# Value products of two key tiles issued together, a third buffer of probabilities, and a new order in the 16-head part of a decoder kernel

## The chip, the cores and the metric

The kernel runs on one core of a Trainium2 chip. A core has TensorE (PE in the rows; its weight loads are PEld), VectorE (DVE), ScalarE (ACT), GpSimd (POOL) and SyncE (SP, which here only issues DMAs); "q" behind an engine's name (SPq) is its sequencer. TensorE writes to PSUM, which has 8 banks of 128 x 512 fp32 words. The metric is the device time of one execution in microseconds (us); lower is better.

## The reference

Eight sequences of 512 tokens, 256 features, go through self attention with 16 heads and rotary positions, cross attention with 16 heads to a second sequence, and two layers of windowed attention with a gated MLP. A layer norm stands behind each of the three. What matters here is the 16-head part:

```python
def _L0_attn_ref(x, w_qkv, w_proj):
    qkv = x @ w_qkv
    qkv = qkv.reshape(B, N, 3, H, hd).transpose(2, 0, 3, 1, 4)
    ...
    q = q * cos + _rotate_half(q) * sin
    k = k * cos + _rotate_half(k) * sin
    attn = jax.nn.softmax(jnp.einsum('bhqd,bhkd->bhqk', q, k) * scale, axis=-1)
    out = jnp.einsum('bhqk,bhkd->bhqd', attn, v)
    ...
x = _layernorm(x + _L0_attn_ref(x, L0_attn_w_qkv, L0_attn_w_proj), axis=-1)
x = _layernorm(x + _L0_xattn_ref(x, ctx_1024, ctx_1024, ...), axis=-1)
x = _layernorm(x + _L0_ffn_ref(x, ...), axis=-1)
```

Heads have 16 features (hd), H is 16, and B here is 8.

## The kernel before

**Stages.** The program is one list of stages (`STAGES`, made by `head_stages` for the 16-head part). Each stage has a function on one or more engines, and every engine runs its own functions in the order of that list. Between engines only semaphores order the work. A "batch" vb is a sequence in the self half (0 to 7, `NB` = 8) or in the cross half (8 to 15).

**One batch.** It has 16 key tiles: four groups g of four heads, times four key tiles kt of 128 keys. For each key tile there are, on TensorE:
- four `amax` matmuls (rows PS<-KS,QS): scores with queries down the partitions, from which VectorE takes the maximum of each query (MX<-PS). They belong to the next batch;
- four `score` matmuls (PS<-QS,KS): the same scores with keys down the partitions and the negated maximum as an added row. ScalarE takes their exponential into the probabilities PT (PT<-PS);
- one `pv`: the value product, four matmuls of 17 columns (16 features and a column of ones for the sum), one for each head, which lie side by side in the array (PS<-PT,VP). The trace lists each twice, since fp32 goes through in two passes. `pv` always writes bank 3. When the fourth key tile of a group is in it, ScalarE copies it to OT (`ot`).

`amax` and `score` have 64 rows each and use different halves of the array, so a pair of them runs at once. Scores run 16 key tiles (`LAG`) behind the maxima: while batch vb's maxima are taken, the scores of vb - 1 run.

**The order.** A step (one batch) has 96 places: 32 slots (half a key tile each) of three. `SELF_ORDER` and `CROSS_ORDER` are tables of (place, stage, part, k): the stage is put at this place of step vb + k. These carry all other work. On TensorE: `tr` (x turned), `rope` and `bias1` (projections of Q and K in halves: L590, 12 matmuls for a half), `val` (L636) and `proj` (L702), 24 matmuls a half, and `maxtr` (maxima turned, L661). The two halves of one projection share two banks: the second half waits until both have "crossed".

**Banks.** `BANKS` is a string of digits: the k-th fill of the 16-head part takes the k-th digit as its bank. A fill waits until the bank's last reader is done (`vacant`, semaphores drained0 to drained7). Bank 3 is `pv`'s, so seven are left.

**Heads.** `rope_out` (or `bias1_out`) copies Q or K from PSUM to the scratch TM. GpSimd turns the rope (`mix`, `mix_sum`). `heads_hi` rounds TM to fp32r in HL, `heads_lo` puts TM - high part beside it in HL. `stack` (SyncE) waits for these, and for the scores of two batches earlier, and spreads high and low parts over QS and KS by 12 DMAs a half in the self part and 6 in the cross part, ahead of them one of NM; it counts rows00 to rows11. `taken` waits for these DMAs. `maxrows` (GpSimd) gathers the maxima, `maxtr` turns them, `negmax` (ScalarE) negates them into NM, `negmax_out` (SyncE) puts them into QS. In the cross half `load_ctx` brings the context, `ctx_hi` (ScalarE) and `ctx_lo` (GpSimd) split it, and `bias1` of K waits for both `ctx_lo`.

**Waits touched.** An exponential of key tile n writes PT[:, kt % 2] and waits for `pv` of n - 2. `rope_out` and `bias1_out` wait for `heads_lo` of the batch before, `heads_hi` waits for its row DMAs (`taken`).

## Time and profile before

| | us |
|---|---|
| median of 3 runs | 2134.76 (2134.24 to 2136.74) |
| the profiled execution | 2138.61 |
| its span, first to last instruction | 2136.8 |
| TensorE busy | 2037.9 (95%) |
| VectorE busy | 1667.7 (78%) |
| ScalarE busy | 1479.9 (69%) |
| GpSimd busy | 1351.0 (63%) |
| mean granted TensorE clock | 0.974 |

The 16-head part runs from the start to about 906 us (the last value product), the rest behind it. A matmul's duration in the rows runs from its start to a modelled end and overlaps the next, so the rate of TensorE is read from starts, not from durations. Idle time of an engine that is not the bottleneck costs nothing.

### The profile page before, as it was taken

To read this page: it belongs to the slowest core of one execution; us is meant where nothing else is said; L and a number is where in the kernel's file an instruction comes from. 1 tells how busy PE (TensorE), PEld (TensorE's weight loads), DVE (VectorE), ACT (ScalarE), POOL (GpSimd) and SP (SyncE) were. 2 spreads that over 40 slices of the span, in tenths; PEclk is the share of its full clock that TensorE was granted. 3 is DMA by queue.
4 is the path that set the end of the run, shared out by engine and by line. 5 is a ranking of instruction groups with operands and counts; after the bars stand their busy time and mean duration, and the time that the engine had idled before them with its cause. 6 is when DMAs were issued, how large, how long until landed. Compare 5 with 4: busy or idle time off the path is not lost.

```text
span 2136.8 us, 47112 instructions
## 1 busy us (share of the span) xinstructions
PE 2037.9 (95%) x15216; PEld 1484.6 (69%) x15216; DVE 1667.7 (78%) x3989; ACT 1479.9 (69%) x3418; POOL 1351.0 (63%) x1378
## 2 busy tenths in 40 slices
PE   5999999999999999779999998999899999999997
PEld 4544555455555554358889897888788988887887
DVE  6888888888888888368888886655488888875775
ACT  2488788888888888737877776554277777775443
POOL 2444566544444442678998885554489888875775
PEclk8799999999999999989999999999999999999999
DMA  4233333333233343446555544200255554551211
GB/s 134 74 101 112 113 103 113 119 119 118 103 119 123 123 123 124 142 96 156 115 120 111 113 108 97 74 16 1 67 111 113 117 118 106 116 116 45 65 60 45
DMA packets 191083, 216.30 MB, mean 101 GB/s; under 512 B 24128, under 2 KB 117056, under 8 KB 190848
## 3 DMA queue, kind: packets, MB, share of 16 engines
q1 hardware_dynamic: 188288, 204.90, 36.4%
q0 software_dynamic: 2560, 8.39, 1.1%
q8 instruction: 133, 2.18, 0.4%
q14 instruction: 102, 0.84, 0.1%
HBM read 47.14 MB, written 29.89 MB: 36 GB/s over the span
## 4 chain that ended last, share of the span: by engine, by line
PE 84%; SPq 4%; DVE 4%; POOL 3%; ACT 2%; issue 2%; DMA 1%; POOLq 0%; ACTq 0%; DVEq 0%
PE PS L685 11%; PE PS L522 11%; PE PS L524 10%; PE PS L523 10%; PE PS L669 10%; PE PS L775 5%; PE PS L799 5%; PE PS L654 5%; PE PS L590 4%; PE PS L784 4%; PE PS L759 2%; SPq L1565 2%; PE PS L702 2%; PE PS L636 2%; SPq L1586 1%
## 5 line engine op out<-in xcount | busy, mean ns | idle before, releaser
L1102 DVE TENSOR_REDUCE MX<-PS 128x1 f32<-128x512 f32 x1024 | 642.9, 683 | 113.3 <-PE PS L654 106.7
L927 ACT ACTIVATE PT<-PS 128x512 f32<-128x512 f32 x1024 | 553.3, 614 | 113.9 <-PE PS L669 111.6
L669 PE MATMUL PS<-QS,KS 64*128 64x512 f32 x1024 | 366.1, 439 | 8.1 <-ACT PT L927 3.5
L654 PE MATMUL PS<-KS,QS 64*128 64x512 f32 x1024 | 353.1, 438 | 7.8 <-DMA KS<-HL 4.8
L669 PEld LDWEIGHTS PS<-QS,KS 64*128 64x128 f32 x1024 | 164.2, 185 | 262.3 <-issue 191.6
L1472 POOL TENSOR_TENSOR PB<-PB,RC 128x512 f32<-128x512 f32 (+1 forms) x256 | 273.4, 1078 | 53.6 <-DVE RC L1224 53.4
L685 PE MATMUL PS<-PT,VP 128*17 128x512 f32 x2048 | 270.3, 600 | 6.7 <-ACT OT L934 5.2
L988 ACT ACTIVATE PB<-PB,NMf 128x256 f32<-128x256 f32 (+1 forms) x512 | 245.4, 490 | 12.7 <-DVE NMf L1215 12.4
L1215 DVE CUSTOM_DVE_ANT_0 PB<-PS,mk 128x256 f32<-128x256 f32 (+1 forms) x512 | 178.3, 386 | 60.9 <-PE PS L775 54.7
L1452 POOL TENSOR_TENSOR RI<-RI,mhalf 128x8 f32<-128x8 f32 x128 | 213.3, 1666 | 10.7
L654 PEld LDWEIGHTS PS<-KS,QS 64*128 64x128 f32 x1024 | 173.3, 189 | 47.5 <-issue 32.1
L775 PE MATMUL PS<-kT,qT 128*128 128x256 f32 (+1 forms) x1024 | 174.8, 294 | 7.8 <-DMA kT<-kT 7.5
L522 PE MATMUL PS<-WQ,XT 128*128 128x512 f32 x384 | 163.1, 425 | 11.5 <-DVE kT L1201 3.8
L524 PE MATMUL PS<-WQ,XT 128*128 128x512 f32 x384 | 155.5, 405 | 0.0
L523 PE MATMUL PS<-WQ,XT 128*128 128x512 f32 x384 | 155.3, 405 | 0.0
L775 PEld LDWEIGHTS PS<-kT,qT 128*128 128x128 f32 x1024 | 141.6, 192 | 16.3 <-issue 7.0
L522 PE MATMUL PS<-HT,W 128*128 128x512 f32 x352 | 142.4, 404 | 1.4 <-POOL HT L1487 0.8
L784 PE MATMUL PS<-ident,PB 128*128 128x128 f32 x896 | 132.0, 275 | 10.9 <-POOL PB L1472 5.9
L524 PE MATMUL PS<-HT,W 128*128 128x512 f32 x352 | 139.4, 396 | 0.0
L523 PE MATMUL PS<-HT,W 128*128 128x512 f32 x352 | 139.3, 396 | 0.0
L1458 POOL TENSOR_TENSOR RA<-RA,RI 128x512 f32<-128x512 f32 x128 | 133.2, 1041 | 3.7 <-DVE RA L1195 3.4
L1000 ACT COPY PTB<-PS 128x512 f32<-128x512 f32 (+1 forms) x256 | 130.6, 543 | 4.9 <-PE PS L784 4.8
(188 smaller groups left out, 4812.9 us busy)
## 6 DMA issues: line engine op xcount, KB each, us to landing
qT<-QN SPq DMA_DIRECT2D x384, 128.0 KB
kT<-kT SPq DMA_DIRECT2D x256, 128.0 KB
od<-OT SPq DMA_DIRECT2D x64, 256.0 KB, 4.0
QS<-HL SPq DMA_DIRECT2D x96, 128.0 KB
KS<-HL SPq DMA_DIRECT2D x96, 128.0 KB
QS<-HL SPq DMA_DIRECT2D x48, 256.0 KB
KS<-HL SPq DMA_DIRECT2D x48, 256.0 KB
OC<-od SPq DMA_DIRECT2D x32, 256.0 KB
```

The lines of the kernel that those rows point to most:

```text
L522: pe.matmul(out, L[0], R[0], start=first, stop=False)
L523: pe.matmul(out, L[0], R[1], start=False, stop=False)
L524: return pe.matmul(out, L[1], R[0], start=False, stop=last)
L654: pe.matmul(PS[:, bank, :], QS[rows, s, h // 2, qt * P:(qt + 1) * P], KS[rows, s, h // 2, :], start=True, stop=True).then_inc(fills("amax" ...
L669: pe.matmul(PS[:, bank, :], KS[rows, s, pair, kt * P:(kt + 1) * P], QS[rows, s, pair, :], start=True, stop=True).then_inc(fills("score", v ...
L685: m = pe.matmul(PS[32 * hh:32 * hh + 17, 3, :], VP[:, vb % 2, kt, 4 * g + hh, :], PT[:, kt % 2, hh, :], start=kt == 0, stop=kt == 3)
L775: m = pe.matmul(out[:, h, k0:], qT[:, u % 2, x, h, hp], kT[:, hp, h, keys], start=x == 0, stop=x == 1)
L784: m = pe.transpose(PS[:, bank, (2 * h + j) * P:(2 * h + j + 1) * P], PB[:, u % 2, 2 * hp + h, j * P:(j + 1) * P], ident[:])
L927: act.activation(PT[:, kt % 2, 2 * i + half], PS[:, TURNS["score", vb, g, kt, half, i][0], :], ACT.Exp).then_inc(drains("score", vb, g, kt ...
L988: m = act.activation(p, p, ACT.Exp, bias=NMf[:, u % 2, hh:hh + 1], scale=-1.0, accum_out=SUM[:, u % 2, hh:hh + 1])
L1102: dve.tensor_reduce(MX[:, vb % 2, h // 8, qt, c:c + 1], PS[:, TURNS["amax", vb, h, qt][0], :], AX, ALU.max).then_inc(drains("amax", vb, h, ...
L1472: pool.tensor_tensor(p, p, RC[:, u % 2, h].unsqueeze(2).broadcast_to([P, 2, 256 - k0]), ALU.mult).then_inc(sem["p_scaled"], 1)
```

## The change

- `pv` of two key tiles now stand together: at every second key tile, behind the first half of its scores, the products of the two tiles before. They were single, each behind the second half of the next tile's scores.
- The probabilities have a third buffer (PT2); the exponential of n waits for `pv` of n - 3.
- The low parts of heads go to TM itself (TMr is the same memory, typed fp32r), HL keeps the high parts alone and is half as large. So `rope_out` (of tile 0) and `bias1_out` wait for the row DMAs of the batch before, instead of `heads_lo`; `heads_hi` no longer does.
- Both order tables and the bank string are new. `load_qkv` also waits for the last `val`.

```diff
+PV_SLOT = 0
...
 SELF_ORDER = (
-    (0, "ot_out", (3,), 2), (2, "val", (1,), 0), (4, "sums", (), 2), (4, "val_out", (0,), 0), (4, "val_out", (1,), 0), (5, "tr", (0,), -1),
+    (1, "rstd", (0,), 4), (2, "stats", (0,), 4), (2, "val_out", (0,), 0), (5, "val_out", (1,), 0), (7, "tr", (0,), -1), (7, "ot", (3,), 2),
...
-            if half and 0 <= n - LAG - 1 < 16 * NV:
-                p = n - LAG - 1
-                out.append(("pv", p // 16, p // 4 % 4, p % 4))
+            if half == PV_SLOT and (n - LAG) % 2 == 0:
+                out += [("pv", p // 16, p // 4 % 4, p % 4) for p in (n - LAG - 2, n - LAG - 1) if 0 <= p < 16 * NV]
...
+            TMr, = aliases(("TMr", [P, 2, 4, S], F32R))
             TM = sb("TM", [P, 2, 4, S], F32)
-            HL = sb("HL", [P, 4, 2, S], F32R)
+            HL = sb("HL", [P, 2, 2, S], F32R)
             xT = sb("xT", [P, 2, 2, S], F32R)
+            PT2 = sb("PT2", [P, 4, S], F32)
...
+        def probs(n):
+            return PT[:, n % 3] if n % 3 < 2 else PT2
...
-                    m = pe.matmul(PS[32 * hh:32 * hh + 17, 3, :], VP[:, vb % 2, kt, 4 * g + hh, :], PT[:, kt % 2, hh, :],
+                    m = pe.matmul(PS[32 * hh:32 * hh + 17, 3, :], VP[:, vb % 2, kt, 4 * g + hh, :], probs(16 * vb + 4 * g + kt)[:, hh, :],
...
             def rope_out(vb, qk, tile):
                 act.wait_ge(*filled("rope", vb, qk, tile))
-                if vb:
-                    act.wait_ge(sem["heads_lo"], n_split(vb - 1, qk, tile))
+                if vb and tile == 0:
+                    taken(act, vb - 1, 0)
...
                 act.wait_ge(*filled("bias1", vb, qk, tile))
-                act.wait_ge(sem["heads_lo"], n_split(vb - 1, qk, tile))
+                taken(act, vb - 1, tile)
...
-                if vb:
-                    taken(act, vb - 1, tile)
-                act.copy(HL[:, 2 * qk + tile, 0], TM[:, qk, tile]).then_inc(sem["heads_hi"], 1)
+                act.copy(HL[:, qk, tile], TM[:, qk, tile]).then_inc(sem["heads_hi"], 1)
...
-                if n >= 2 and half == 0 and i == 0:
-                    act.wait_ge(sem["pv"], n - 1)
+                if n >= 3 and half == 0 and i == 0:
+                    act.wait_ge(sem["pv"], n - 2)
...
             def mix(vb, qk, tile):
-                if vb == 1 and qk == 0 and tile == 0:
-                    pool.wait_ge(sem["heads_lo"], 4)
...
-                pool.tensor_tensor(HL[:, hb, 1], TM[:, qk, tile], f(HL[:, hb, 0]), ALU.subtract).then_inc(sem["heads_lo"], 1)
+                pool.tensor_tensor(TMr[:, qk, tile], TM[:, qk, tile], f(HL[:, qk, tile]), ALU.subtract).then_inc(sem["heads_lo"], 1)
...
                     for tile in range(2):
                         taken(sp, NV - 1, tile)
+                    for half in range(2):
+                        sp.wait_ge(*filled("val", NV - 1, half))
```

The big pieces that a table moves are shown by what stands in a row on an engine. On TensorE, in a stretch of batch 5 that holds nothing but scores, maxima and products, before (L669 is a score, L654 a maxima, L685 a product; drainedN is the wait for bank N):

```order
L685 MATMUL PS<-PT,VP 17x512 [waits s_drained7,s_drained5,s_drained4,s_drained0]
L685 MATMUL PS<-PT,VP 17x512 x3
L669 MATMUL PS<-QS,KS 128x512 [waits s_negmax_in,s_drained0]
L654 MATMUL PS<-KS,QS 128x512 [waits s_drained4,s_rows00]
L669 MATMUL PS<-QS,KS 128x512 [waits s_negmax_in,s_drained1]
L654 MATMUL PS<-KS,QS 128x512 [waits s_drained6,s_rows00]
L654 MATMUL PS<-KS,QS 128x512 [waits s_drained7,s_rows00]
L669 MATMUL PS<-QS,KS 128x512 [waits s_negmax_in,s_drained2]
L654 MATMUL PS<-KS,QS 128x512 [waits s_drained5,s_rows00]
L669 MATMUL PS<-QS,KS 128x512 [waits s_negmax_in,s_drained0]
L685 MATMUL PS<-PT,VP 17x512 [waits s_drained6,s_drained2,s_drained4]
L685 MATMUL PS<-PT,VP 17x512 x3
```

The same kind of stretch in the changed kernel, in the cross half (L674, L659, L690 are the same three), its last eight fills (eight more stand ahead of them) and the products:

```order
L659 MATMUL PS<-KS,QS 128x512 [waits s_drained1,s_rows10]
L674 MATMUL PS<-QS,KS 128x512 [waits s_negmax_in,s_drained2]
L659 MATMUL PS<-KS,QS 128x512 [waits s_drained6,s_rows10]
L674 MATMUL PS<-QS,KS 128x512 [waits s_negmax_in,s_drained4]
L674 MATMUL PS<-QS,KS 128x512 [waits s_negmax_in,s_drained7]
L659 MATMUL PS<-KS,QS 128x512 [waits s_drained0,s_rows11]
L674 MATMUL PS<-QS,KS 128x512 [waits s_negmax_in,s_drained5]
L659 MATMUL PS<-KS,QS 128x512 [waits s_drained2,s_rows11]
L690 MATMUL PS<-PT2,VP 17x512 [waits s_drained5,s_drained2,s_drained0,s_drained7]
L690 MATMUL PS<-PT2,VP 17x512 x3
L690 MATMUL PS<-PT,VP 17x512 [waits s_drained2,s_drained4,s_drained0]
L690 MATMUL PS<-PT,VP 17x512 x3
```

Eight fills stood between two visits of the value products, and now sixteen stand between two double visits.

On GpSimd, in the middle of a cross step, before (xT<-tab is `ctx_lo`, MB is `maxrows`):

```order
L1378 TENSOR_TENSOR xT<-tab,xT 128x512 [waits s_x_hi] x2
L1399 TENSOR_TENSOR OCr<-OC,OCr 128x512 [waits s_oc_hi]
L1387 CAST MB<-MX 128x8x4 [waits s_drained6,s_drained7,s_drained2,s_drained5,s_drained4,s_filled0,s_drained1,s_drained0]
L1389 TENSOR_TENSOR MB<-MX,MB 128x8x4 [waits s_max_parts]
L1374 TENSOR_TENSOR HL<-TM,HL 128x512 [waits s_heads_hi] x2
```

and in the changed kernel:

```order
L1377 TENSOR_TENSOR xT<-tab,xT 128x512 [waits s_x_hi]
L1386 CAST MB<-MX 128x8x4 [waits s_drained7,s_drained4,s_drained6,s_drained0,s_drained2,s_filled0,s_drained5,s_drained1]
L1388 TENSOR_TENSOR MB<-MX,MB 128x8x4 [waits s_max_parts]
L1377 TENSOR_TENSOR xT<-tab,xT 128x512 [waits s_x_hi]
L1398 TENSOR_TENSOR OCr<-OC,OCr 128x512 [waits s_oc_hi]
```

The gathering of the maxima, which stood behind both low parts of the context, now stands between them.

On SyncE, in a cross step, before (QS<-NM of L1595 and the rows behind it are `stack` of the first half, QS<-NM of L1603 is `negmax_out`):

```order
L1610 DMA od<-OT 128x512 [waits s_sums_in,s_oc_in,s_ot]
L1595 DMA QS<-NM 4x4x512 [waits s_filled5,s_heads_lo]
L1588 DMA QS<-HL 32x4x512 x3
L1588 DMA KS<-HL 32x4x512 x3
L1603 DMA QS<-NM 4x4x512 [waits s_drained6]
L1610 DMA od<-OT 128x512 [waits s_ot] x2
L1573 DMA tab<-ctxT 128x2x512 [waits s_ctx_lo]
```

and in the changed kernel (L1594 begins `stack` there, L1602 is `negmax_out`; the first row shown is that of the second half of the maxima):

```order
L1602 DMA QS<-NM 4x4x512 [waits s_drained0]
L1572 DMA tab<-ctxT 128x2x512 [waits s_ctx_lo]
L1617 DMA OC<-od 128x1x512 [waits s_oc_lo,s_ot_out1,s_ot_out0]
L1609 DMA od<-OT 128x512 [waits s_sums_in,s_oc_in,s_ot]
L1631 DMA rs<-RR 128x64 [waits s_recip_in,s_recip_rows]
L1602 DMA QS<-NM 4x4x512 [waits s_drained4]
L1594 DMA QS<-NM 4x4x512 [waits s_filled1,s_heads_lo]
L1587 DMA QS<-HL 32x4x512 x2
L1587 DMA QS<-TMr 32x4x512
L1587 DMA KS<-HL 32x4x512
L1587 DMA KS<-TMr 32x4x512
L1587 DMA KS<-HL 32x4x512
```

The rows of the first half now stand behind `negmax_out` of the first half, and the context's load behind `negmax_out` of the second.

## Rows read from the trace of the kernel before

**Rows 1.** The page: busy time of TensorE, and the chain that ended last.

```profile
PE 2037.9 (95%) x15216; PEld 1484.6 (69%) x15216; DVE 1667.7 (78%) x3989; ACT 1479.9 (69%) x3418; POOL 1351.0 (63%) x1378
...
PE 84%; SPq 4%; DVE 4%; POOL 3%; ACT 2%; issue 2%; DMA 1%; POOLq 0%; ACTq 0%; DVEq 0%
```

**Rows 2.** Windows: stretch, length, busy PE, PEld, DVE, ACT, POOL (count), PEclk, DMA.

```profile
344.60:397.50 52.90, 52.21 (x428) 27.26 (x424) 44.51 (x78) 44.30 (x90) 35.34 (x36) 1.00 0.37 112
603.90:655.10 51.20, 51.03 (x428) 26.88 (x424) 44.05 (x77) 44.67 (x88) 22.99 (x26) 1.00 0.38 117
130.00:850.00 720.00, 715.06 (x5772) 368.26 (x5770) 615.81 (x1054) 611.80 (x1214) 346.63 (x372) 1.00 0.37 116
```

**Rows 3.** Timeline of TensorE, one bare key tile: start, duration, engine, line, tiles.

```profile
366.88 1.05 PE L685 MATMUL PS<-PT,VP 128*17 128x512 f32 x8
367.86 0.50 PE L669 MATMUL PS<-QS,KS 64*128 64x512 f32 x1
...
368.20 0.39 PE L669 MATMUL PS<-QS,KS 64*128 64x512 f32 x1
...
368.44 0.39 PE L669 MATMUL PS<-QS,KS 64*128 64x512 f32 x1
...
369.05 0.50 PE L669 MATMUL PS<-QS,KS 64*128 64x512 f32 x1
369.48 1.05 PE L685 MATMUL PS<-PT,VP 128*17 128x512 f32 x8
```

**Rows 4.** Timeline of TensorE, a key tile with half a projection.

```profile
382.80 1.05 PE L685 MATMUL PS<-PT,VP 128*17 128x512 f32 x8
...
384.36 1.60 PE L702 MATMUL PS<-WO,OCr 64*128 64x256 f32 x24
...
386.02 0.39 PE L669 MATMUL PS<-QS,KS 64*128 64x512 f32 x1
386.34 1.05 PE L685 MATMUL PS<-PT,VP 128*17 128x512 f32 x8
```

**Rows 5.** Timelines of VectorE and of ScalarE in the bare key tile.

```profile
368.43 2.48 DVE L1102 TENSOR_REDUCE MX<-PS 128x1 f32<-128x512 f32 x4 [0.23 <-PE PS L654]
...
368.39 2.06 ACT L927 ACTIVATE PT<-PS 128x512 f32<-128x512 f32 x4 [0.24 <-PE PS L669]
```

**Rows 6.** Groups, 130 to 850 us: count, busy, mean ns, idle before them.

```profile
L1102 DVE TENSOR_REDUCE MX<-PS 128x1 f32<-128x512 f32 x893 | 561.9, 683 | 91.0 <-PE PS L654 85.1
L927 ACT ACTIVATE PT<-PS 128x512 f32<-128x512 f32 x894 | 484.6, 612 | 89.1 <-PE PS L669 86.8
...
L934 ACT COPY OT<-PS 128x512 f32<-128x512 f32 x56 | 33.1, 591 | 4.0 <-PE PS L685 0.8
...
L1130 DVE BATCH_NORM_STATS2 LNT<-X 128x6 f32<-128x256 f32 x48 | 17.8, 414 | 0.0
...
L1072 DVE TENSOR_TENSOR xT<-PS,xT 128x512 fp32r<-128x512 f32 x26 | 16.8, 686 | 7.9 <-ACT xT L872 7.9
```

**Rows 7.** Timelines of SyncE and ScalarE, start of a self step.

```profile
238.38 0.58 SPq L1595 DMA_DIRECT2D QS<-NM  x1
...
242.83 4.35 SPq L1586 DMA_DIRECT2D KS<-HL  x6
...
252.27 0.60 ACT L884 ACTIVATE TM<-PS 128x512 f32<-128x512 f32 x1 [0.45 <-PE PS L590]
```

**Rows 8.** Timeline of GpSimd, middle of a cross step.

```profile
629.81 1.28 POOL L1378 TENSOR_TENSOR xT<-tab,xT 128x512 fp32r<-128x512 f32 x1 [3.49 <-ACT xT L878]
...
631.33 0.26 POOL L1389 TENSOR_TENSOR MB<-MX,MB 128x32 fp32r<-128x32 f32 x1
```

**Rows 9.** Timelines of SyncE and TensorE, end of a cross step.

```profile
539.78 0.60 SPq L1595 DMA_DIRECT2D QS<-NM  x1
...
542.35 1.92 SPq L1588 DMA_DIRECT2D KS<-HL  x3
...
552.30 0.49 PE L654 MATMUL PS<-KS,QS 64*128 64x512 f32 x1
```

**Rows 10.** The page's DMA issues: KB each, median us to landing.

```profile
od<-OT SPq DMA_DIRECT2D x64, 256.0 KB, 4.0
```

100 lines of the change are left out of this document (49 added, 51 removed).

## The prediction

> **What bounds the kernel now.** I read the page first. TensorE is busy for 95% of the span, and 84% of the chain that ended last is its own work [rows 1]. The change touches only the 16-head part, so the next view is its steady stretch. From 130 to 850 us TensorE shows 715.06 of 720 us busy, at the full granted clock (1.00, the 2.4 GHz level), while VectorE has 615.81 and ScalarE 611.80 [rows 2]. "Busy" here hides waiting, so starts have to be read. One key tile of four heads is four score matmuls, four matmuls for the maxima, and one value product. In a key tile with nothing else on TensorE, products start at 366.88 and at 369.48: 2.60 us [rows 3]. The work in it is less: a pair (score and maxima, half the rows each) starts 0.24 us after the one before (368.20, 368.44), so four pairs are 0.92; the products keep the array for 0.87 (two passes). That is 1.79, and 0.81 is something else. About 0.28 of it is changing over: 0.09 before the products (386.02 + 0.23 to 386.34, [rows 4]) and 0.19 behind them (366.88 + 0.87 to 367.86 is 0.11; the pair that starts there holds its place for 0.34 instead of 0.23, [rows 3]). The remaining 0.53 is a PSUM wait: seven banks serve eight fills, so the last score (369.05) needs the bank of the first (367.86), which is free when its exponential has ended, 368.39 + 0.60 = 368.99 [rows 3, 5]. VectorE is full in such a tile as well: four maxima in 2.48 us, 0.60 apart [rows 5].
>
> In a key tile that also holds half a projection (24 matmuls, 1.4 us) the period is 382.80 to 386.34, 3.54 us: 1.79 + 1.38 + 0.37, with no bank wait [rows 4]. So there are two regimes. A bare tile is bound by banks, VectorE and ScalarE; a loaded one by TensorE, and there the idle time of the other two collects (91.0 and 89.1 us of the 720, [rows 6]). The stretch has 893 / 4 = 223 key tiles [rows 6]; the whole part has 256. A batch took 52.90 us in the self half and 51.20 in the cross half [rows 2].
>
> **Value products of two tiles together.** 256 visits become 128, so 128 changeovers of 0.28 us go, 36 us, if TensorE is the bound everywhere. In loaded stretches it is. In bare ones I walk the new chain, with t = 0 at the first pair behind a double burst. Fills are ready at 0.50; exponentials then leave every 0.49, maxima every 0.60 [rows 5]. Sixteen fills share seven banks. By the new order the fifteenth takes the bank of the eighth (the fourth maxima: 0.54 + 3 x 0.60 + 0.68 = 3.02), the sixteenth that of the tenth (the fifth exponential: 3.10). The last pair is out at 3.2; then 0.43 to the products (369.05 to 369.48, [rows 3]), 0.98 + 0.87 for both: 5.48 us for two tiles, against 5.20 now. So a bare pair of tiles loses 0.28 where a loaded pair wins 0.28 or more. A pair with one projection half now takes 3.54 + 2.60 = 6.14 and needs only 5.5. Nothing has to be hidden for the third buffer itself: it has the 8 KB a partition that the halved HL gives up, and the exponential of tile n now waits for products n - 3.
>
> **The order anew.** It decides how much of each kind there is. I cut a batch's step into the eight stretches between double bursts and took for each the largest of: TensorE's work + 0.37; ScalarE's (0.49 an exponential, 0.5 to 0.6 any other, by the 0.59 of OT); VectorE's (0.60 a maxima, 0.65 a low part, by 0.69 less overlap, 1.05 a statistics stage, two of 0.41 and two shorter); and the 5.48. [Rows 5, 6] carry these. Self step: 9.7 + 6.1 + 5.5 + 5.5 + 5.5 + 6.9 + 6.7 + 8.2 = 54. Cross step: 6.5 + 6.7 + 5.5 + 6.7 + 5.5 + 6.9 + 5.8 + 6.7 = 50.2. The same rule on the old order, tile by tile with 2.60 as the floor, gives 52.6 (row: 52.90) and 52.2 (row: 51.20). In the self step the 8.2 is VectorE with both statistics stages and both low parts of x behind one another, and next to it stand three rope halves on TensorE (9.7) in which VectorE has only 4.8; work spills over such a border, up to the banks, so I take off 1.5. That makes self batches 52.5 against 52.9, say -0.3 each for five of them. For the cross half and the mixed steps before it the rule says -2.0; I take -1.3 because of the waits of the next paragraph. Eight of these; the first two steps and the last have few such stretches and count 0.
>
> **Steps that are moved.** The low parts of heads go to TM (TMr), so rope_out and bias1_out wait for the row DMAs of the batch before, which they did not. In a self step the second half's rows are issued from 238.38 to 247.18, and the old first rope_out stood at 252.27 [rows 7]. The new one stands some three places later, behind the burst, so the wait is met: cost 0; without that cover up to 2 us a batch. Heads_hi loses the same wait: 0, it was met long before. In a cross step GpSimd now does maxrows(0) between the two ctx_lo: these took 1.28 us, maxrows about 0.5 [rows 8]. It cannot start before the 32nd maxima. By the stretches above the burst at the batch's middle starts 6.7 + 6.5 + 6.7 + 5.5 = 25.4 us into it, and VectorE is some 1.9 behind there: 27.3. So ctx_lo(1) ends at 27.3 + 0.5 + 1.3 = 29.1, where bias1 of K is due at 28.8 (the burst and six pairs): 0.3 us, between 0 and 1 a batch. TensorE waits there, and the score fills behind it. On SyncE negmax_out(0) now stands ahead of stack(0), which earlier went 39 us into the batch (539.78 to 544.27) with the first maxima of the next at 552.30 [rows 9]. Now it waits for maxtr(0): the last two stretches, 6.9 + 5.8, less the burst and two pairs (2.4) and the negation behind two exponentials (1.3), so about 9 us before the next batch; then 0.6 and 4.5 us of issues, and a store takes up to 4.0 to land [rows 10]: between 1.3 us to spare and 0.6 late, I take 0.2. Both together 0.5, rounded up to 0.7 for the later load_ctx behind negmax_out(1). The two waits of load_qkv for val cost 0: by its place that val is some 40 us old by then. Everything behind the 16-head part stands in the old order with the same tiles: 0.
>
> **The sum.** 5 x -0.3 + 8 x -1.3 = -12 us. The profiled execution took 2138.6 us (span 2136.8 and 1.8 around it), 3.9 above the median of 2134.76, so I put the difference on the median: **2123 us**.
>
> **The rivals.** (A) *TensorE's whole saving shows*: work spills freely over the borders, the 0.28 comes back 128 times, with some bank wait saved too: -24 to -40, about 2103. For it: in the loaded tiles nothing but TensorE binds [rows 4]. Against it: VectorE is full in the bare ones [rows 5]. The Trainium skill, TensorEngine Tiling (Array Packing), Key Properties, says that changing the tiling mode drains TensorE; by that rule alone this rival would be the forecast, and the trace agrees with the drain but not that it binds everywhere. (B) *The evacuation takes it back*: during a burst of 1.85 us no score is made. At its second product at most two exponentials are queued (0.98 us) against 1.5 us until the next, and VectorE's queue is 3.5 of 0.60. Bare pairs pay 0.28 four times a batch, and the crowded 8.2 stretch does not spill: self +1.3 x 5; cross (-1.3 + 4 x 0.5) x 8, where in each of four light stretches one more step of VectorE or ScalarE, 0.5 us, falls in front of the last bank: +12, 2147. It decides from the point at which a double stretch with no projection takes over 5.8 us. The same page, section PSUM Bottleneck, warns that the PSUM copy may become the limit once TensorE is faster; no figure of it is used. (C) *Late rows or late context*: TensorE waits 2.5 us instead of 0.7 in each cross batch, because GpSimd and SyncE are blocked as above (8 x (-2.0 + 2.5) = +4), and the self rows are late by 1 us (5 x (-0.3 + 1.0) = +3.5): +8, 2143. (D) *No change*: gains and losses cancel within 4.3 us.
>
> **How the numbers follow.** The forecast, -4.3 to -24: 0.48. A: 0.12. D: 0.15. B: 0.15. C: 0.10. Faster by over 0.2% (4.3 us, about what a measurement of this kernel can tell) is 0.60, within it 0.15, slower 0.25. The range is 2103 to 2147: A's middle to B; the forecast's own is 2111 to 2130.
>
> **What would show it.** After: 128 bursts of products, each 1.92 us from its first to its last matmul's end, with no gap between the two tiles (a gap would mean that exponentials are late). Bare stretches of 5.4 to 5.6 us from burst to burst; over 5.8 says B. Loaded ones of 6.6 to 6.9 with two projection halves. Cross batches near 50, self near 52.5. TensorE waiting for xT of GpSimd, or for KS and QS by DMA, for more than 5 us in all says C. What follows 906 us should take as long as before. If bare stretches stay at 5.2, the bank chain is wrong and it is A.

## The result, and the profile after

The changed kernel took 2174.48 us (median of 4 runs, 2171.94 to 2177.27) against 2135.75 us for the kernel before beside it (4 runs, 2134.24 to 2142.25): ratio 1.0179, 95% interval 1.016 to 1.0198. It is slower, by 38.7 us. The prediction of 2123 us had the sign wrong, and its range ended at 2147.

**Where the time went.** I looked first for the stage. In the kernel before, the last value product starts at 905.5 us and 1231 us follow to the end. In the changed kernel it starts at 945.6 us and 1230 us follow. So all of the loss lies in the 16-head part, and what stands behind it cost nothing, as predicted. Inside that part the first maxima of each batch give its length. In the order of the batches:

| us | self, 1 to 3 | 4 to 7 | 8 (mixed) | 9 (first context) | cross, 10 on |
|---|---|---|---|---|---|
| before | 44.8, 51.6, 51.7 | 54.4, 53.0, 52.8, 53.0 | 51.3 | 51.9 | 51.6, 51.6, 51.2, 51.5, 51.4, 51.5 |
| after | 45.9, 52.2, 53.6 | 57.3, 55.1, 55.0, 55.1 | 53.2 | 57.0 | 54.7, 54.0, 54.2, 54.1, 54.1, 54.2 |

Nearly every batch is 2 to 3 us longer, and one is 5 us longer. The loss is spread out, so it has a cause that returns in each batch.

The page after (busy time, then the share of the chain that ended last, by engine; then groups with their idle time):

```profile
PE 2062.3 (95%) x15216; PEld 1536.5 (71%) x15216; DVE 1663.1 (76%) x3989; ACT 1474.0 (68%) x3418; POOL 1350.7 (62%) x1378
...
PE 77%; DVE 5%; SPq 5%; ACT 3%; POOL 3%; DMA 3%; issue 3%; POOLq 0%; DVEq 0%; ACTq 0%
...
L1104 DVE TENSOR_REDUCE MX<-PS 128x1 f32<-128x512 f32 x1024 | 636.2, 681 | 165.1 <-PE PS L659 164.0
L930 ACT ACTIVATE PT<-PS 128x512 f32<-128x512 f32 x1024 | 550.8, 616 | 162.2 <-PE PS L674 161.7
```

Set beside [rows 1], TensorE is "busy" for 24 us more with the same instructions, its own work is 77% of the chain instead of 84%, and transfers have 3% instead of 1%. VectorE and ScalarE have as much work as before; they only wait longer for TensorE.

The windows that answer to [rows 2] (a self batch, a cross batch, the steady stretch; the columns are those of that group):

```profile
356.10:411.30 55.20, 54.08 (x426) 31.15 (x426) 44.29 (x77) 44.22 (x90) 35.27 (x37) 1.00 0.38 111
630.10:684.20 54.10, 52.53 (x424) 29.88 (x424) 44.38 (x78) 44.27 (x89) 23.03 (x26) 1.00 0.33 112
130.00:890.00 760.00, 737.78 (x5781) 416.67 (x5779) 610.22 (x1053) 605.31 (x1212) 346.03 (x372) 1.00 0.35 111
```

The granted clock is 1.00 here as in [rows 2], so the clock has no part in it.

**A bare double stretch** (timeline of TensorE, changed kernel: two key tiles with nothing else, from burst to burst; some rows left out):

```profile
652.66 1.91 PE L690 MATMUL PS<-PT,VP 128*17 128x512 f32 x16
654.50 0.49 PE L659 MATMUL PS<-KS,QS 64*128 64x512 f32 x1
...
655.31 0.39 PE L674 MATMUL PS<-QS,KS 64*128 64x512 f32 x1
655.81 0.59 PE L659 MATMUL PS<-KS,QS 64*128 64x512 f32 x2
...
657.77 0.47 PE L659 MATMUL PS<-KS,QS 64*128 64x512 f32 x1
658.17 0.62 PE L690 MATMUL PS<-PT,VP 128*17 128x512 f32 x4
```

The burst is 1.91 us for 16 passes in one piece, 1.92 was predicted. The stretch is 5.51 us, 5.48 was predicted. The step that I had worked hardest on was right, and it is a loss, as predicted: two bare tiles of the kernel before take 5.19 us.

**A loaded double stretch** (same view, two halves of a projection of 24 matmuls each, L641):

```profile
630.73 1.91 PE L690 MATMUL PS<-PT,VP 128*17 128x512 f32 x16
632.57 0.49 PE L659 MATMUL PS<-KS,QS 64*128 64x512 f32 x1
...
633.14 0.62 PE L674 MATMUL PS<-QS,KS 64*128 64x512 f32 x2
633.88 0.47 PE L659 MATMUL PS<-KS,QS 64*128 64x512 f32 x1
634.37 1.70 PE L641 MATMUL PS<-W,xT 64*128 64x256 f32 x24
635.88 0.39 PE L659 MATMUL PS<-KS,QS 64*128 64x512 f32 x1
...
636.34 1.61 PE L641 MATMUL PS<-W,xT 64*128 64x256 f32 x24
...
638.34 0.62 PE L690 MATMUL PS<-PT,VP 128*17 128x512 f32 x4
```

This one takes 7.61 us, where 6.5 to 6.9 was predicted. Read the starts: the burst and its exit take 1.84 us (to 632.57). Eight fills follow. The first pair holds its place for 0.34 us (632.57 to 632.91), three more need 0.23 each, so the projection could start 1.03 us later. It starts 1.80 us later, at 634.37. The eighth fill comes at 633.88 instead of 633.37, and the projection waits again, since it needs two banks at once. That is 0.77 us in which TensorE has no bank to write to. Behind the first half of the projection nothing waits any more: 1.51, 0.46, 1.41, 0.46 and 0.13 us. In the kernel before a projection half stood behind four fills and did not wait at all ([rows 4]: 382.80 + 0.98 + two pairs, and L702 is there at 384.36).

VectorE in the same stretch (its timeline; the bracket is the idle time before the row):

```profile
628.57 3.67 DVE L1104 TENSOR_REDUCE MX<-PS 128x1 f32<-128x512 f32 x6
...
633.10 2.48 DVE L1104 TENSOR_REDUCE MX<-PS 128x1 f32<-128x512 f32 x4
...
636.30 1.29 DVE L1104 TENSOR_REDUCE MX<-PS 128x1 f32<-128x512 f32 x2 [0.71 <-PE PS L659]
```

and ScalarE:

```profile
628.84 2.58 ACT L930 ACTIVATE PT<-PS 128x512 f32<-128x512 f32 x5
633.14 2.06 ACT L930 ACTIVATE PT<-PS 128x512 f32<-128x512 f32 x4 [1.72 <-PE PS L674]
...
636.33 1.09 ACT L930 ACTIVATE PT<-PS 128x512 f32<-128x512 f32 x2 [0.65 <-PE PS L674]
```

ScalarE has emptied its queue 0.7 us after the burst began (628.84 + 2.58 = 631.42) and idles 1.72 us. From 633.14 on it gives back a bank every 0.49 us. By the bank string the eighth fill takes the bank of the first exponential, which ends at about 633.74 (633.14 + 0.60), and the fill starts at 633.88. The projection takes the banks of the first maxima (its matmul at 632.57) and of the second exponential, which ends at about 634.23, and it starts at 634.37. So both waits end with ScalarE's first two exponentials behind the burst. VectorE isn't idle there: the rows left out at 632.15 to 633.11 are statistics. Later, during the projections, both engines idle again.

**Against the kernel before, kind by kind.** The loaded stretches are where the forecast was missed, but they aren't the only place where the change lost. In a cross batch two tiles with a half of `val` each took 7.1 to 7.3 us and now take 7.6 together. The two halves of `proj` with a `maxtr` took 7.3 to 7.8 and take 7.8. The tiles with the projections of Q and K lose 0.4 in all, those with `tr` and `maxtr` 0.5, and the three bare pairs 0.3 each, which the prediction had counted. With late rows (next) that makes the 2.4 to 3.1 us of a cross batch. A pair of tiles thus costs 0.3 us in the mean (38.7 / 128).

**Late rows, cross half** (timeline of SyncE, changed kernel, the end of a batch):

```profile
675.18 0.57 SPq L1602 DMA_DIRECT2D QS<-NM  x1
675.85 0.56 SPq L1594 DMA_DIRECT2D QS<-NM  x1
...
679.69 1.32 SPq L1587 DMA_DIRECT2D KS<-HL  x1
```

and the first maxima of the next batch on TensorE:

```profile
684.24 0.50 PE L659 MATMUL PS<-KS,QS 64*128 64x512 f32 x1 [0.44 <-DMA KS<-HL]
```

`stack` of the first half is issued from 675.85, behind `negmax_out`; its last issue ends at 681.0, and the row of TensorE says that a transfer of these rows is what it waited for until 684.24. The fill before it stood at 683.3, so 0.9 us passed without one. At the starts of batches 11 to 16 these gaps are 0.8 to 1.5 us, at that of batch 10 2.1. (With rows in time, in e8 below, they are 0.3, and 0.5 at batch 10.)

In the self half the rows are in time, but the negated maxima are not: `negmax_out` stands behind the twelve issues of `stack`. Before 465 us TensorE waits for QS<-NM by DMA 3.3 us in six times, and the last double stretch of the self batches takes 8.0 to 8.7 us, where the same work takes 7.6 in the cross half.

### The profile page after: what moved, and what is told of

The parts are those of the page before. It is cut to its first block, busy times and chain, and to the rows that moved or that the text cites. A ratio compares the mean times of both kernels' runs of the same rounds, so it can differ in the third digit from the quotient of the medians.

```text
span 2175.5 us, 47041 instructions
## 1 busy us (share of the span) xinstructions
PE 2062.3 (95%) x15216; PEld 1536.5 (71%) x15216; DVE 1663.1 (76%) x3989; ACT 1474.0 (68%) x3418; POOL 1350.7 (62%) x1378
## 4 chain that ended last, share of the span: by engine, by line
PE 77%; DVE 5%; SPq 5%; ACT 3%; POOL 3%; DMA 3%; issue 3%; POOLq 0%; DVEq 0%; ACTq 0%
PE PS L527 11%; PE PS L528 10%; PE PS L529 10%; PE PS L690 9%; PE PS L659 7%; PE PS L674 5%; PE PS L780 5%; PE PS L804 5%; PE PS L595 4%; PE PS L789 4%; PE PS L764 2%; SPq L1585 2%; DVE MX L1104 2%; DMA KS<-HL 2%; PE PS L641 2%
## 5 line engine op out<-in xcount | busy, mean ns | idle before, releaser
L1104 DVE TENSOR_REDUCE MX<-PS 128x1 f32<-128x512 f32 x1024 | 636.2, 681 | 165.1 <-PE PS L659 164.0
L659 PE MATMUL PS<-KS,QS 64*128 64x512 f32 x1024 | 375.4, 447 | 19.2 <-DMA KS<-HL 6.3
L674 PE MATMUL PS<-QS,KS 64*128 64x512 f32 x1024 | 353.8, 437 | 6.0 <-DMA QS<-NM 5.0
L659 PEld LDWEIGHTS PS<-KS,QS 64*128 64x128 f32 x1024 | 175.6, 188 | 189.1 <-issue 170.2
L690 PE MATMUL PS<-PT,VP 128*17 128x512 f32 x2048 | 249.0, 602 | 8.5 <-ACT OT L937 4.6
L674 PEld LDWEIGHTS PS<-QS,KS 64*128 64x128 f32 x1024 | 171.7, 184 | 57.2 <-issue 14.2
L690 PEld LDWEIGHTS PS<-PT,VP 128*17 128x17 f32 x2048 | 48.0, 96 | 126.4 <-issue 108.3
```

Of the source, the lines that this page charges most:

```text
L659: pe.matmul(PS[:, bank, :], QS[rows, s, h // 2, qt * P:(qt + 1) * P], KS[rows, s, h // 2, :], start=True, stop=True).then_inc(fills("amax" ...
L674: pe.matmul(PS[:, bank, :], KS[rows, s, pair, kt * P:(kt + 1) * P], QS[rows, s, pair, :], start=True, stop=True).then_inc(fills("score", v ...
L690: m = pe.matmul(PS[32 * hh:32 * hh + 17, 3, :], VP[:, vb % 2, kt, 4 * g + hh, :], probs(16 * vb + 4 * g + kt)[:, hh, :], start=kt == 0, st ...
L1104: dve.tensor_reduce(MX[:, vb % 2, h // 8, qt, c:c + 1], PS[:, TURNS["amax", vb, h, qt][0], :], AX, ALU.max).then_inc(drains("amax", vb, h, ...
```

## The experiments

All times are medians, and each ratio is to the kernel before, run on the same chip beside it. The kernel before gave 2134.5 to 2137.1 us beside them, so a difference of two experiments is known to some 3 us; where it matters, the difference by the ratios is given too. The first four cross the two parts: order tables (with their bank string), and products alone or together. All four keep the new layout, the third buffer and the new waits.

### Old order, single products (e1)

```diff
 SELF_ORDER, CROSS_ORDER, BANKS: those of the kernel before
-            if half == PV_SLOT and (n - LAG) % 2 == 0:
-                out += [("pv", ...) for p in (n - LAG - 2, n - LAG - 1) ...]
+            if half and 0 <= n - LAG - 1 < 16 * NV:
+                p = n - LAG - 1
+                out.append(("pv", p // 16, p // 4 % 4, p % 4))
```

> The order tables and the bank string of before, each value product alone, but the third buffer, the low parts over TM and their waits as in the changed kernel. Theory (the waits for PSUM banks behind a double burst cost the time): nothing but waits with room differs from before, so the time is that of before, 2131 to 2139 us. Rival (the wait of rope_out and bias1_out for the row DMAs costs it): 15 us or more above before, since in the old order the first rope_out stands some 2 us behind the landing.

Measured: 2158.22 us, 1.0104 (1.0083 to 1.0125), above what I expected: the rival was right, though through `bias1_out` alone. From the fourth to the eleventh the batches are as before; then come 56.6, 57.8, 55.7 and 57.2 us instead of 51.2 to 51.5. The waits of ScalarE from 600 to 828 us (what waited, for whom: us in total, times, longest):

```profile
ACT TM L898 <- DMA KS<-HL: 14.6, 4, 4.3
```

and those of TensorE in the same stretch:

```profile
PE PS L660 <- ACT TM L898: 14.3, 4, 4.2
```

L898 is `bias1_out` and L660 the maxima. The new layout makes it wait for the rows of the second half, which the old table issues late (`stack`(1) at place 9). The self batches from the fourth on do not change, so the wait of `rope_out` costs nothing there (the first three are 3.9 us shorter together, which I did not follow up). But my "0" for the layout held only with the new table.

### The same, with one issue moved (e5)

```diff
-(9, "stack", (1,), 0)
+(0, "stack", (1,), 0)
```

> Kernel: the two order tables, the bank string and the single value products of the kernel before, with the third buffer, the new place of the low parts and the new waits of the change; only stack(1) of the cross half goes from place 9 to place 0, so that the row transfers that bias1_out now waits for are issued some 5 us earlier. Theory (the layout costs nothing in itself; the +21 us of e1 were those late rows alone, which e1 showed as 14.6 us of waiting in 4 batches at ScalarE and as four last batches of 55.7 to 57.7 us instead of 51.5): 2137 us, between 2133 and 2142, all cross batches at 51.2 to 51.9. Rival (third buffer or the new waits of heads_hi, rope_out and bias1_out cost in every batch): 2150 or more. A third buffer that helps the single products by sparing a wait would give below 2130.

Measured: 2136.93 us, 1.0018 (1.0007 to 1.0029), as expected. One entry of the table gives back 18 us by the ratios (21 by the medians). The third buffer wins nothing for single products, and the layout costs next to nothing: the self batches from the second on have 51.0 to 54.4 us, as before or up to 0.6 less, and of the cross batches one has 53.9 and the last two 52.2 and 52.3, where `bias1_out` still waits a little for rows (TensorE waits for it 2.7 us in five times).

### Old order, products together (e2)

```diff
 SELF_ORDER, CROSS_ORDER, BANKS: those of the kernel before (products together as changed)
```

> The order tables and the bank string of before, with the value products of two key tiles together. Theory: the pairing by itself costs, because four pairs of matmuls and then a projection half follow a burst and meet seven banks: 2150 to 2185 us, with loaded stretches of 7.4 us or more. Rival (the new order costs it and the pairing gains): below before, 2105 to 2125 us.

Measured: 2303.21 us, 1.0779 (1.0759 to 1.0798), far outside of both expectations. A stretch of it (TensorE):

```profile
631.24 1.91 PE L690 MATMUL PS<-PT,VP 128*17 128x512 f32 x16
633.08 1.69 PE L707 MATMUL PS<-WO,OCr 64*128 64x256 f32 x24
...
635.80 0.47 PE L659 MATMUL PS<-KS,QS 64*128 64x512 f32 x1 [0.34 <-ACT PT L930]
...
636.42 1.77 PE L707 MATMUL PS<-WO,OCr 64*128 64x256 f32 x24
...
640.81 0.62 PE L690 MATMUL PS<-PT,VP 128*17 128x512 f32 x4
```

Here the projection stands directly behind the burst: from the burst's start no score or maxima is made for 3.4 us, and already the sixth fill behind it waits for a bank. From burst to burst it is 9.57 us for the same work and one `maxtr`, where the changed kernel takes 7.8. So a projection right behind a burst looks worse than one behind eight fills; tables and bank string differ as well, and its place was not varied alone. The new tables avoid that place; they were made for the pairs.

### New order, single products (e3)

```diff
 products as in the kernel before, and two ot entries later, behind their last product:
-(49, "ot", (1,), 1)    # self        -(26, "ot", (0,), 1)    # cross
+(54, "ot", (1,), 1)                  +(30, "ot", (0,), 1)
```

> The order tables and the bank string of the changed kernel, with each value product alone behind the second half of the next tile's scores; two entries of ot (self 1 from 49 to 54, cross 0 from 26 to 30) stand later, so that ScalarE doesn't wait for products that come later. Theory: with the bursts apart the bank waits shorten, and what is left over before are late rows in the cross half and the crowded VectorE stretch: 2140 to 2160 us. Rival (the new order is what costs): as slow as the changed kernel, 2168 us or more.

Measured: 2217.28 us, 1.0377 (1.0361 to 1.0392): a miss for the theory, the rival's side of it (2168 or more). TensorE again:

```profile
635.33 1.05 PE L691 MATMUL PS<-PT,VP 128*17 128x512 f32 x8 [1.06 <-ACT OT L938]
...
639.01 0.50 PE L675 MATMUL PS<-QS,KS 64*128 64x512 f32 x1 [0.36 <-DVE MX L1105]
```

The products wait for `ot`, 12.6 us in 13 times from 130 to 890 us, fills wait for banks another 27 us, and both halves of a projection often fall into one single tile. So the four combinations are: old order 2158 (2137 with the one entry moved) single and 2303 together; new order 2217 single and 2174 together. Each table fits its own way of placing the products, and the two halves of the change can't be added up. That says nothing yet on the pairing itself.

### Rows ahead of negmax_out (e4)

```diff
-(49, "negmax_out", (0,), 0), (50, "stack", (0,), -1)
+(79, "negmax_out", (0,), 0), (50, "stack", (0,), -1)
```

> The changed kernel with one entry moved: in the cross half negmax_out of the first half stands behind stack of the first half on SyncE (place 79 instead of 49). Theory: the first maxima of a cross batch start in the changed kernel as the rows land (684.24 us), so each of eight batches is freed of 0.5 to 1.5 us: 2162 to 2171 us. If rows are the main cause it falls to 2150 or less; if they cost nothing it stays within 3 us of 2174.

Measured: 2186.03 us, 1.0223 (1.0204 to 1.0241): a miss. The rows came in time, but the negated maxima now came behind them in SyncE's queue (waits of TensorE, 470 to 700 us):

```profile
PE PS L674 <- DMA QS<-NM: 10.7, 3, 4.5
```

It moved the lateness from one transfer to the other, and three batches around the start of the cross half became 58.7 to 59.7 us.

### Smaller rows (e8)

```diff
-                        sp.dma_start(f(T[k:P:4, vb % 2, pairs]), f((HL, TMr)[a][:, qk, half]))...
+                        few, rows = (pairs, slice(0, P)) if k < 2 else (slice(4 * half, 4 * half + 1), slice(0, 32))
+                        sp.dma_start(f(T[k:P:4, vb % 2, few]), f((HL, TMr)[a][rows, qk, half]))...
```

> The changed kernel, in which of the six row transfers of a cross half (256 KB each) the third and the sixth bring 32 KB rather than 256 (a quarter of the pairs, a quarter of the rows): a part of the operands is left out, the issues on SyncE stay. Theory (in the cross batches the rows of the next batch land too late: stack(0) is issued 45.7 to 50.9 us into the batch and lands at 54.1, where the first maxima of the next stands): 0.5 to 1.3 us less in each of 8 cross batches: 2163 to 2171 us, and TensorE's waits for KS and QS by DMA (11.4 us in 15 times) fall below 4. Rival (what ends the batch is TensorE's own time and the rows only come last by a hair): 2172 or more.

Measured: 2167.44 us, 1.0159 (1.014 to 1.0179), as expected: 7.0 us less than the changed kernel by the medians, 4.3 by the ratios, whose intervals overlap. The traces decide for the larger number: the 16-head part is 7.1 us shorter (938.5 against 945.6 us to the last product). The waits of TensorE for KS by DMA (4.5 us, and 6.9 at its weight loads) are gone but for 0.3. The batch of the first context goes from 57.0 to 53.9, the cross batches from 54.1 to 53.8. So late rows are about 7 us of the 38.7, and some 32 are left.

### Half the evacuation (e6, e7)

VectorE and ScalarE read 256 of the 512 columns in each maxima and each exponential: half of the evacuation of PSUM is left out, TensorE's work stays. e6 is the kernel before with it, e7 the changed one.

```diff
-dve.tensor_reduce(MX[...], PS[:, TURNS["amax", vb, h, qt][0], :], AX, ALU.max)
+dve.tensor_reduce(MX[...], PS[:, TURNS["amax", vb, h, qt][0], 0:256], AX, ALU.max)
...
+                w = S if n < 3 else 256
-                act.activation(probs(n)[:, 2 * i + half], PS[:, ..., :], ACT.Exp)
+                act.activation(probs(n)[:, 2 * i + half, 0:w], PS[:, ..., 0:w], ACT.Exp)
```

> Kernel before, in which each maxima (VectorE) and, from the third key tile on, each exponential (ScalarE) reads 256 of the 512 columns of its bank; half of the probabilities stay those of the first tiles. It leaves out half of this work on the two engines and nothing on TensorE. It is the partner of e7. A maxima should come every 0.33 us instead of 0.60 (the 128x256 statistics take 0.41 where 128x512 takes 0.68) and an exponential every 0.27 instead of 0.49. The bank wait of 0.53 in each bare key tile goes: some 90 to 130 tiles of 0.3 to 0.5 us, so -35 to -60: 2075 to 2100.

> The changed kernel with the same work left out as in e6 (half of each maxima and of each exponential). Theory (in a double burst VectorE and ScalarE empty their queues, and afterwards the banks come back at their pace, which makes the loaded double stretches 7.6 us long instead of 6.7 to 6.9): with both twice as fast the loaded stretches fall to 6.5 to 6.9, the bare ones to 4.2 to 4.8, and of the 38.7 us between the two kernels at most 15 remain: 2090 to 2115 us, a gain of 60 to 85 against the changed kernel. Rival (TensorE itself, its projections behind eight fills or the order, takes the 7.6): loaded stretches stay above 7.3, and the distance to e6 stays 30 us or more.

Measured: e6 2102.51 us (0.9852, 0.9835 to 0.9869), a little above its range; e7 2113.96 us (0.9895, 0.9869 to 0.992), as expected. The changed kernel gains 60 us from it, the kernel before 32, and of the 38.7 us between the two 11.5 are left. So most of what the change lost hangs on how fast banks come back, and not on TensorE's own work. The readers are not quite twice as fast: an exponential comes every 0.28 us instead of 0.49, a maxima every 0.34 to 0.37 instead of 0.60.

Stretch by stretch the pair says more. In the cross half two tiles with a half of `val` each take 3.54 + 3.54 us in e6 and 7.18 together in e7, `proj` with its `maxtr` 7.5 to 7.8 and 7.48, two bare tiles 4.76 and 4.61. So with faster readers pairing costs at most 0.1 us in a stretch, and in most it wins. What keeps e7 behind e6 is transfers, for which TensorE waits 22.5 us in 14 times (130 to 890 us), in e6 3.5 in three. The rows of e7:

```profile
PE PS L674 <- DMA QS<-NM: 11.6, 7, 2.7
PE PS L659 <- DMA KS<-HL: 10.9, 7, 2.0
```

The loaded stretch in e7 (TensorE):

```profile
557.92 1.91 PE L690 MATMUL PS<-PT,VP 128*17 128x512 f32 x16
559.76 0.50 PE L659 MATMUL PS<-KS,QS 64*128 64x512 f32 x1
...
560.92 0.47 PE L659 MATMUL PS<-KS,QS 64*128 64x512 f32 x1
561.20 1.66 PE L595 MATMUL PS<-xT,W 64*128 64x512 f32 x12
...
565.10 0.62 PE L690 MATMUL PS<-PT,VP 128*17 128x512 f32 x4
```

From burst to burst it is 7.18 us, where I had set at most 6.9. From the first fill to the projection it is 1.44 us instead of 1.80. So 0.41 of the 0.77 us of waiting is left. This looks like the way round the loop rather than the rate: the first bank can only come back when its matmul has written, the reader has started and the reader has ended. In [rows 3, 5] that is 368.99 - 367.86 = 1.13 us, while the eighth fill could go 0.80 us behind the first (632.57 to 633.37). After a burst ScalarE's queue is empty, so this has to be paid from the start each time.

The Trainium skill, TensorEngine Tiling (Array Packing), section PSUM Bottleneck, says that tiling speeds TensorE up but not the evacuation of PSUM, whose copies may become the bottleneck. This pair of runs agrees: with half of the evacuation left out the kernel before gains 32 us and the changed one 60.

### Pairs in some places only (e9 to e12)

Kernel e5 with products together in a part of the tiles. e9: in tiles where no projection is (40 pairs); e10: in tiles where one is (56 pairs). Order and bank string stay. The burst stands in the tile behind its pair, so the two are less pure than their names: 8 of the bursts of e9 are followed by one or two halves of a projection, and 19 of those of e10 by none.

```diff
+PAIRED = ((0, 0, 1, 1, 1, 0, 0, 0), (0, 0, 1, 1, 0, 0, 0, 0))     # e9; e10: ((1, 1, 0, 0, 0, 0, 1, 1), (1, 0, 0, 0, 1, 0, 0, 1))
...
+                    pair = PAIRED[p >= 16 * NB][p % 16 // 2]
+                    if half == (n - LAG) % 2 == 0 if pair else half == 1 and p == n - LAG - 1:
+                        out.append(("pv", p // 16, p // 4 % 4, p % 4))
```

> Kernel e5 (orders and single products of before, new layout, 2136.9 us) in which only some key tiles have their products together: in the self half the tiles 4 to 9 of each batch, in the cross half 4 to 7, as 3 and 2 pairs; 40 pairs in all. They lie where no projection stands. Nothing else moves, the bank string neither. By the step of the prediction (a bare pair of tiles takes 5.48 instead of 5.20): +0.28 each, +11: 2148 us. The changed kernel's bare double stretches took 5.50 to 5.59, 0.3 to 0.4 more than two single tiles; since this order was not made for pairs, up to 0.8 each: 2148 to 2170. Rival (TensorE's changeovers are what counts everywhere): -0.28 each, 2126.

> Kernel e5 again, with the products together where projections stand: tiles 0 to 3 and 12 to 15 in the self half, 0, 1, 8, 9, 14 and 15 in the cross half, 4 and 3 pairs a batch, 56 in all, nothing else moved. By the step of the prediction (TensorE binds there, and each pair saves one changeover): -0.28 each, -16: 2121 us. New theory (the burst lets VectorE and ScalarE run dry, and then TensorE, which has projections and eight fills to place, waits for banks; the changed kernel's loaded stretches are 0.9 us over the predicted 6.7): +0.9 to +1.3 each, +50 to +73: 2187 to 2210 us, that is several times what the bare pairs cost.

Measured: e9 2182.25 us (1.0214, 1.0197 to 1.023), e10 2215.52 us (1.0378, 1.0361 to 1.0395). Both lie above what I expected. Against e5 that is +45 us for 40 bare pairs, 1.1 us each, and +79 us for 56 loaded ones, 1.4 us each (42 and 77 us by the ratios). The loaded pairs cost more, but not several times more, and the bare ones cost far more than the 0.28 of the prediction's step. In the mean no kind of pair gains anything in this order, and both cost some four times the 0.3 us that a pair costs in the changed kernel, whose order was made for pairs. VectorE in a bare pair of e9:

```profile
658.66 4.87 DVE L1108 TENSOR_REDUCE MX<-PS 128x1 f32<-128x512 f32 x8 [1.67 <-PE PS L663]
```

It stands idle for 1.67 us, then does its eight maxima without a gap, and the stretch is 5.99 us (656.28 to 662.27). In the changed kernel's bare stretch (burst at 652.66) it reads

```profile
652.54 1.29 DVE L1104 TENSOR_REDUCE MX<-PS 128x1 f32<-128x512 f32 x2 [0.62 <-PE PS L659]
655.04 3.08 DVE L1104 TENSOR_REDUCE MX<-PS 128x1 f32<-128x512 f32 x5 [1.21 <-PE PS L659]
```

There VectorE has work until 1.17 us into the burst, idles 1.21, and the stretch is 5.51. So it looks as if the work queued at the start of a burst decides; no run varied that alone.

TensorE also waited for banks of maxima in e9 (3.6 us in 20 times), so I renewed the bank string alone: each fill takes the bank that has been free longest.

> Kernel e9 (products together in 40 places without projections, 2182.3 us) with another bank string and nothing else: each fill takes the bank that has been free longest in this order. In e9 a bare double stretch took 5.99 us with two waits for banks of maxima in it, in the changed kernel 5.50 without. Theory (about half of e9's +45 is the string, the rest the pairing): -0.3 to -0.6 a pair, 2158 to 2170 us. Rival (the string has no part): 2178 or more. If pairing bare tiles cost only its own 0.3 a pair, it would be 2149.

> Kernel e10 (products together in 56 places with projections, 2215.5 us) with a bank string renewed in the same way and nothing else. Theory (here the queues run dry, and no choice of bank helps, since all are free after the burst and none is a moment later): 2200 to 2212 us, so still over 1.1 us a pair. Rival (as for e11, the string is half of it): 2175 to 2190.

Measured: e11 2179.64 us (1.0204, 1.0187 to 1.0221), e12 2221.02 us (1.04, 1.0385 to 1.0416). My theory for e11 fell: the string has no part worth naming (-3 us where -12 to -24 was expected); the same bare stretch is 6.02 us (657.28 to 663.30), now with a wait of 0.21 for an exponential's bank in place of one for a maxima's. e12 was even 5.5 us slower than e10, above its range. Which bank is taken matters little here, how many there are is the same.

### Both ways with new tables (e13, e14)

Other places in both tables, each started from its kernel's own, and a bank string to match. e13 is the changed kernel (all products together), e14 is e5 (single). The projections move by 0 to 2 places; some 230 of the 292 entries of the four tables move. Those of e13 that bear on the rows:

```diff
-(53, "stack", (0,), -1)  (56, "negmax_out", (0,), 0)     # self
+(47, "stack", (0,), -1)  (49, "negmax_out", (0,), 0)
...
-(49, "negmax_out", (0,), 0)  (50, "stack", (0,), -1)     # cross
+(56, "negmax_out", (0,), 0)  (44, "stack", (0,), -1)
```

> The changed kernel with all products together, third buffer and layout as it has them, and with other places in both order tables, on all engines (projections by 0 to 3 places, SyncE's, GpSimd's, ScalarE's and VectorE's steps by more), and a bank string to match. Theory (late rows go, some 1 us a cross batch, and some of the self half's waits; the loaded stretches stay over 7 us): 2150 to 2165 us. Rival (the loss of the changed kernel was one of its tables, pairing wins when it is ordered well): 2137 or less.

> Kernel e5 (single products, third buffer, new layout, 2136.9 us) with other places in both tables, found in the same way as for e13 from the tables of before, and a bank string to match. If the third buffer and freer waits leave anything to win, it is in the tiles that hold two things: 2120 to 2132 us. Rival (the tables of before are at their floor): 2134 to 2140.

Measured: e13 2163.69 us (1.0134, 1.0117 to 1.0152), 10.8 us better than the changed kernel (9.6 by the ratios), as the theory said. The late rows are gone (TensorE's list of waits from 130 to 890 us holds no transfer any more), and a cross batch is 53.7 us. Its stretches are 7.6, 6.6, 7.6, 5.5, 7.5, 5.5, 7.8 and 5.5 us, the changed kernel's 7.6, 6.7, 7.6, 5.5, 7.5, 5.5, 7.8 and 5.9. With most entries elsewhere these loaded ones did not move. In the self half the last stretch fell from 8.0 to 8.7 us to 7.61, as in the cross half, with the negated maxima in time. A loaded one (TensorE):

```profile
637.05 0.49 PE L656 MATMUL PS<-KS,QS 64*128 64x512 f32 x1
...
638.42 0.46 PE L656 MATMUL PS<-KS,QS 64*128 64x512 f32 x1 [0.17 <-ACT PT L927]
638.91 1.67 PE L592 MATMUL PS<-xT,W 64*128 64x512 f32 x12
```

From the first fill to the projection it is 1.86 us, the changed kernel's 1.80 again.

e14 missed: 2156.11 us (1.0094, 1.0079 to 1.0109), slower than e5 and than the kernel before, where 2120 to 2132 was expected. One batch has 59.3 us. TensorE's largest wait, once for 4.7 us, is for an exponential:

```profile
PE PS L657 <- ACT PT L928: 6.4, 6, 4.7
```

and ScalarE, on which that exponential was queued, waited for a scaled output of GpSimd:

```profile
ACT OCr L939 <- POOL OC L1392: 5.3, 1, 5.3
```

The other cross batches are 52.1 to 52.3 instead of 51.2 to 51.6. Products together with tables of their own thus end 27 us (25 by the ratios) behind single products with the old tables and one moved entry (e5). Whether a still better table for pairs exists was not shown; none of those tried came within 1.3% of the kernel before, and no run that does all of the work beat it.

## Why the prediction was wrong

By its steps:

- **What bounds the kernel before: right in kind.** The two regimes, the clock, and the part behind the 16 heads stood as read. One sum is off: the changeover behind the products is 0.11 + (0.34 - 0.23) = 0.22, not 0.19, so a visit costs 0.31 us and the bank wait of a bare tile is 0.50. It changes nothing below.
- **The burst and the bare double stretch: right.** 1.91 us in one piece (1.92 predicted), and 5.50 to 5.59 us (5.48 predicted).
- **The loaded double stretch: this step failed.** I took TensorE's work + 0.37, the excess that one loaded tile had in [rows 4]. The two-projection-half stretches of a cross batch took 7.6, 7.6, 7.5 and 7.8 us, work + 1.2 to 1.26. Two single tiles have work + 0.74 together, so pairing them was to win 0.37 and lost up to 0.6. In a single tile only 0.98 us of products and four fills stand ahead of the projection, and it does not wait. With 1.84 us of products and eight fills ahead of it, it does. I had walked the chain of banks for the bare stretch and not for the loaded one, where I called TensorE the bound and stopped. The difference is 30.5 - 27.0 = 3.5 us in each cross batch, 28 us for the eight, and in the self batches 10.1, 7.8 and 8.0 to 8.7 instead of 9.7 (the prediction says three rope halves, the table has four, and the 9.7 is for four), 6.9 and 6.7, another 2.6 us, 13 us for the five. Some 4 of the 13 are the late negated maxima, in the stretch put at 6.7. So 37 of the 51 us between -12 and +38.7 are this step, and late transfers another 11. The measured cause of the excess is the wait for banks: 0.77 us in the row, ended by ScalarE's first two exponentials, and with faster readers (e6, e7) pairing costs at most 0.1 us in such a stretch.
- **The crowded self stretch: about right.** The one that I had put at 8.2 took 6.7; the 1.5 us that I had taken off for work that spills over a border was about what went.
- **Rows of the cross half: mis-sized.** I had put 0.2 us a batch, between 1.3 to spare and 0.6 late. Fills stopped for 0.8 to 1.5 us at the start of the cross batches, and for 2.1 at the first one. e8 gives about 7 us for all. The transfers came 3.2 us after the end of their last issue, within my 4.0 (which in [rows 10] is a median, not the most). But `negmax_out` stood only 8.1 us ahead of the time at which TensorE could have gone on (675.18, and 683.3), not 9, and the issues of `stack` took 5.2 us (675.85 to 681.01), not 4.5.
- **Negated maxima of the self half: a term that I had left out.** `negmax_out` stands behind the twelve issues of `stack` there, and the last stretch, which waits for it, is 0.4 to 1.1 us longer in each batch than the 7.61 of e13.
- **ctx_lo(1) behind maxrows(0): not separated.** No row shows `bias1` waiting for it, and nothing was run on it alone.
- **The waits of rope_out and heads_hi at 0: right** for the self half (e1, e5). For `bias1_out` the 0 hung on the table: with the old one it was 14.6 us.
- **The rivals.** B named the right mechanism, evacuation, at the wrong place: it was to decide from the point at which a bare stretch takes over 5.8 us. They took 5.5, and the loss that the forecast lacked was in the loaded ones, where I had seen nothing but gain. C was right in kind (TensorE waited for KS and QS by DMA for 7.8 us, and 6.9 at its weight loads), but in the self half the negated maxima were late and not the rows. A, that TensorE's saving shows in full, was furthest off. The Trainium skill, TensorEngine Tiling (Array Packing), Key Properties, says that changing the mode drains TensorE; a gap is there (0.09 us in, 0.11 us out behind it), and to save 128 of them is worth something only where TensorE is not about to wait for a bank.
- **The range** left out that the term of the loaded stretches could be wrong in all of its some 50 places at once. Its upper end was built from 0.5 us in each of the light stretches alone.

## What to carry to other kernels

Grouping work of one kind saves changeovers, but it also makes the time in which the producer fills no buffer longer. Ask how long the readers' queues last at that moment (here 0.7 us for ScalarE and 0.7 to 1.5 for VectorE, against a burst of 1.84) and walk the chain of buffers afterwards for the stretches with the most other work, not only for the empty ones: there a bank wait comes on top of the producer's own work. Look at the empty ones too: here they lost what had been predicted for them. An order table and a grouping are fitted to each other, so test a part of such a change in a table that suits it, and look at every transfer whose issue a new wait now hangs on.

## What I had not expected of the hardware

- Three buffers instead of two for the probabilities bought nothing for single products (e5, 1.0018), though an exponential could then run a tile further ahead. Half of the evacuation of PSUM left out gave 32 us (e6), so it is the banks that limit rather than this buffer.
- Reading half of the columns did not halve what the loop costs: a bare key tile went from 2.60 to 2.38 us only (e6). An exponential every 0.28 us instead of 0.49 leaves the way from a matmul to its reader's start as it was (0.53 us in [rows 3, 5]).
- How much the place of a projection behind a burst matters: the stretch that held two halves and one `maxtr` took 9.57 us with the first half directly behind the burst (e2) and 7.8 us with it behind eight fills (changed kernel); only the tables and their bank string differ between the two kernels.
